# A decoder in one kernel: layer 1's attention with four PSUM banks for maxima and two for scores in place of three and three

## The reference, cut to what matters

```python
qkv = hidden_states @ Wqkv_w.T + Wqkv_b          # b, s, (3, H, HD)
q, k, v = (qkv[:, :, 0], qkv[:, :, 1], qkv[:, :, 2])
softmax_scale = 1.0 / np.float32(np.sqrt(HD))
scores = jnp.einsum('bthd,bshd->bhts', q, k) * softmax_scale
attn = jax.nn.softmax(scores, axis=-1)
ctx = jnp.einsum('bhts,bshd->bthd', attn, v)
return ctx.reshape(b, s, d) @ out_w.T + out_b
```

## Time and profile before

| | us |
|---|---|
| median of 3 runs | 2740.32 |
| lowest and highest | 2739.88, 2743.84 |
| profiled execution, in all | 2736.73 |
| its span | 2735.0 |
| layer 1's attention in it | 1158 to 1461 |
| TensorE busy, share of the span | 2459.4, 90% |
| VectorE busy | 1747.2, 64% |
| ScalarE busy | 1212.6, 44% |

### The profile page before, as it was taken

The page is one execution under the profiler, slowest core; times in us unless marked ns, Lnnn a source line. Parts: engine busy times, 40 slices in busy tenths (PEclk is TensorE's granted clock), DMA queues, the critical chain, the costliest instruction groups (busy, mean ns, idle before and its releaser), DMA issues. The chain is left out here.

```text
span 2735.0 us, 39447 instructions
## 1 busy us (share of the span) xinstructions
PE 2459.4 (90%) x11412; PEld 1779.8 (65%) x11412; DVE 1747.2 (64%) x3684; ACT 1212.6 (44%) x2343; POOL 157.9 (6%) x265
## 2 busy tenths in 40 slices
PE   7999977679999769899999599999999999999579
PEld 5554445457777657654446477777777777777457
DVE  6677756668888662266664666676667666666643
ACT  3566654223333332266663344444444444444321
POOL 0000000010000000100003101010100101010100
PEclk9999998879999979989999799999999999999789
DMA  5522100000000023343320100000000000000101
GB/s 164 167 70 69 52 0 0 17 1 1 0 0 0 4 102 114 120 112 92 84 54 0 54 9 19 4 15 4 15 12 8 12 12 15 4 8 0 40 1 62
DMA packets 71459, 103.69 MB, mean 38 GB/s; under 512 B 14447, under 2 KB 27514, under 8 KB 71262
## 3 DMA queue, kind: packets, MB, share of 16 engines
q1 hardware_dynamic: 71390, 102.82, 12.8%
HBM read 72.90 MB, written 29.88 MB: 38 GB/s over the span
## 5 line engine op out<-in xcount | busy, mean ns | idle before, releaser
L2673 DVE SCALAR_TENSOR_TENSOR x_res<-xa_out_bank,xa_den,x_res 128x512 f32 (+1 forms) x256 | 191.5, 748 | 157.2 <-PE xa_out_bank L2313 157.2
L2582 ACT ACTIVATE xa_pT_hi<-xa_t_bank 128x512 fp32r<-128x512 f32 x256 | 149.5, 597 | 124.8 <-PE xa_t_bank L2450 124.8
L2593 ACT ACTIVATE xa_prob<-xa_prob,xa_nmax 128x512 f32<-128x512 f32 x256 | 182.9, 717 | 30.0 <-DVE xa_nmax L2655 30.0
L2313 PE MATMUL xa_out_bank<-xa_o_w,xa_o_hi 128*128 128x512 f32 x512 | 173.1, 419 | 22.5 <-DVE x_res L2673 20.9
L2637 DVE TENSOR_TENSOR xa_pT_lo<-xa_t_bank,xa_pT_hi 128x512 fp32r<-128x512 f32 x256 | 175.7, 687 | 22.7 <-ACT xa_pT_hi L2582 18.6
L2655 DVE CUSTOM_DVE_ANT_0 xa_prob<-xa_s_bank,xa_mask_bias 128x512 f32<-128x512 f32 x256 | 171.1, 687 | 20.1 <-PE xa_s_bank L2313 10.1
L585 DVE TENSOR_REDUCE l1s_mx<-l1s_max_bank 128x1 f32<-128x512 f32 x256 | 156.3, 682 | 13.2 <-PE l1s_max_bank L447 13.2
L1722 DVE SCALAR_TENSOR_TENSOR ffn_yT<-ffn_y,ffn_ysc,ffn_yT 128x512 f32<-128x512 f32 x176 | 129.3, 748 | 48.9 <-PE ffn_y L1494 48.7
L585 DVE TENSOR_REDUCE l0s_mx<-l0s_max_bank 128x1 f32<-128x512 f32 x256 | 156.0, 682 | 2.8 <-PE l0s_max_bank L447 2.7
L2450 PE MATMUL xa_t_bank<-ident,xa_prob 128*128 128x128 f32 x1024 | 149.8, 274 | 0.1
L572 ACT ACTIVATE l1s_pT<-l1s_score_bank 128x512 f32<-128x512 f32 x256 | 140.0, 601 | 16.3 <-PE l1s_score_bank L466 14.8
(11 more groups left out here) (447 smaller groups left out, 5905.9 us busy)
## 6 DMA issues: line engine op xcount, KB each, us to landing
l0s_q<-l_q SPq DMA_DIRECT2D x96, 128.0 KB, 2.4
l1s_q<-l_q SPq DMA_DIRECT2D x96, 128.0 KB, 3.1
l1s_k<-l_k SPq DMA_DIRECT2D x96, 128.0 KB, 3.3
l0s_k<-l_k SPq DMA_DIRECT2D x96, 64.0 KB, 2.4
x_res<-in_x_dram SPq DMA_DIRECT2D x4, 1024.0 KB, 9.8
l_q<-l_q_hi SPq DMA_DIRECT2D x16, 256.0 KB, 2.6
l_q<-l_q_lo SPq DMA_DIRECT2D x16, 256.0 KB, 3.3
l_q<-l1p_hi SPq DMA_DIRECT2D x16, 256.0 KB, 2.1
```

What stands on the lines that cost most here:

```text
L2313: last = pe.matmul(bank, w, x, start=(m == 0), stop=(m == len(pairs) - 1))
L2582: act.activation(pT_hi[:, kt % (QT - 1), :], t_bank[kt % 2][:], ACT.Copy).then_inc(pT_hi_done, 1)
L2593: act.activation(prob[:, q, :], prob[:, q, :], ACT.Exp, bias=nmax[:, q:q + 1], scale=-1.0, accum_out=den[:, r, 0, q:q + 1]).then_inc(exp_d ...
L2673: dve.scalar_tensor_tensor(xt, out_bank[:], den[:, r, 2, q:q + 1], xt, ALU.mult, ALU.add)\
```

## The change

`PairAttention` gets a number `maxima`, three unless told otherwise; layer 1's attention passes four. It has that many maxima banks and six less that many score banks. Each wait follows its own number: a maximum now waits for the reduction `NM` before it, a score for the exponential `NS` before it. The bank of product j is (8s + j) mod the number of banks, the same as before for three. Layer 0's attention keeps three and three, and the eight banks of PSUM are all in use as before. No instruction is added or removed.

```diff
-    def __init__(self, st, stack, name, q_dram, k_dram, v, per_head, out):
+    def __init__(self, st, stack, name, q_dram, k_dram, v, per_head, out, maxima=3):
...
-        self.max_bank = [ps(f"{name}_max_bank{g}", [P, S]) for g in range(3)]
-        self.score_bank = [ps(f"{name}_score_bank{g}", [P, S]) for g in range(3)]
+        self.NM, self.NS = maxima, 6 - maxima
+        self.max_bank = [ps(f"{name}_max_bank{g}", [P, S]) for g in range(self.NM)]
+        self.score_bank = [ps(f"{name}_score_bank{g}", [P, S]) for g in range(self.NS)]
...
-        reached(pe, self.max_read, 8 * p + j - 2)
-        pe.matmul(self.max_bank[(2 * s + j) % 3][:], self.qs[s][0:self.STK, n, q * P:(q + 1) * P],
+        reached(pe, self.max_read, 8 * p + j - self.NM + 1)
+        pe.matmul(self.max_bank[(8 * s + j) % self.NM][:], self.qs[s][0:self.STK, n, q * P:(q + 1) * P],
...
-        reached(pe, self.exp_done, 8 * p + k - 2)
-        pe.matmul(self.score_bank[(2 * s + k) % 3][:], self.ks[s][0:self.STK + 2, n % self.KN, kt * P:(kt + 1) * P],
+        reached(pe, self.exp_done, 8 * p + k - self.NS + 1)
+        pe.matmul(self.score_bank[(8 * s + k) % self.NS][:], self.ks[s][0:self.STK + 2, n % self.KN, kt * P:(kt + 1) * P],
...
-                act.activation(self.pT[:, n, kt, :], self.score_bank[(2 * s + k) % 3][:], ACT.Exp, scale=HD ** -0.5)\
+                act.activation(self.pT[:, n, kt, :], self.score_bank[(8 * s + k) % self.NS][:], ACT.Exp, scale=HD ** -0.5)\
...
-        dve.tensor_reduce(self.mx[:, j // QT, j % QT:j % QT + 1], self.max_bank[(2 * s + j) % 3][:], AX.X, ALU.max)\
+        dve.tensor_reduce(self.mx[:, j // QT, j % QT:j % QT + 1], self.max_bank[(8 * s + j) % self.NM][:], AX.X, ALU.max)\
...
-        att = PairAttention(st, stack, name, q_dram, k_dram, v, per_head, out)
+        att = PairAttention(st, stack, name, q_dram, k_dram, v, per_head, out, maxima=4)
```

## The result

The changed kernel takes 2747.7 us (median of 10 runs, 2744.2 to 2751.1) against 2740.8 for the kernel before (10 runs, 2738.9 to 2744.0): ratio 1.0025, 95% interval 1.0016 to 1.0034. That is 6.9 us (4.4 to 9.3) slower. The forecast was 2742.5, within 2737 to 2748; the time lies at the range's upper end.

A forecast was written before the change was run, and what follows sets the result against it. The prediction took TensorE's own order as the bound, held in layer 1's loop by maxima waiting for VectorE's reductions. Its terms -1.0+1.4+0.5+1.75-0.4 = +2.2 us, added to the median 2740.32, gave 2742.5 us, range 2737 to 2748.

The forecast's parts named there:

- The wait moves from maxima to scores: Loop steps: maxima's waits for VectorE go or become small; two to three held score loads per step, 1.5 us or less.
- The chain of the two score banks: Steady steps: held load 0.64 us after an exponential's start, next exponential 0.535 later; score 7 starts 3.865 after the first exponential.
- Steps 6 to 29: Layer 1 attention's hardware loop: removed stall replaced almost exactly, -0.04 us a step, -1.0 in all.
- Steps 2 to 5: Layer 1 attention's steps with constant numbers: last score starts at 3.865 for 3.50 us, +0.35 each, +1.4 in all.
- Step 1: Layer 1 attention's step where nothing has to be turned first: last score starts later, +0.5 us.
- The start: Start of layer 1's attention: maximum 7 of pair 1 waits one reduction less, -0.60 to -0.30 us, taken as -0.4.
- Steps 30 and 31: Layer 1 attention's last two steps, without maxima: two score banks delay the last score, +0.87 us each, +1.75 in all.
- The sum: Whole kernel: -1.0+1.4+0.5+1.75-0.4 = +2.2 us, giving 2742.5 us.
- The rival that the stall really goes: Steps with maxima: scores do not bind, -0.59 us in 24 loop steps, about -16 us, 2724; chance 0.03.
- The rival by the clock: Steps 30 and 31: TensorE's clock falls again after looser score stretches; one fall +3.9 us, two +5.6, 2746; chance 0.08.
- The range: Whole kernel's time: 2737 to 2748 us, allowing 3 us for another median.

The follow-up runs named there:

- e9b_half_exp_42: Changed kernel (four maxima, two score banks) with half of layer 1's exponentials left out, 256 of 512 columns; -14.8 us against the kernel before.
- e10b_half_exp_33: Three maxima and three score banks, with half of layer 1's exponentials left out, 256 of 512 columns; -2.5 us against the kernel before.
- e1_after_again: The changed kernel unaltered, run and profiled a second time; +6.3 us against the kernel before.
- e1b_new_text_33: The changed kernel's text with three maxima and three score banks in layer 1, as in the kernel before; -0.2 us against the kernel before.
- e11_filled_tail_42: Changed kernel with sixteen unread matmuls added for TensorE in steps 30 and 31, into idle maxima banks; +2.4 us against the kernel before.
- e5_fixed_tile_42: Changed kernel with layer 1's division written to a fixed-address tile and copied on later by VectorE; +5.6 us against the kernel before.
- e7_six_tail_42: Changed kernel with the scores of steps 30 and 31 put into all six maxima and score banks; -1.5 us against the kernel before.
- e4_fixed_tile_33: Three and three banks, with layer 1's division written to a fixed-address tile and copied on later by VectorE; -6.6 us against the kernel before.

## Why the prediction was partly right and where it failed

- *The wait moves from maxima to scores.* Right, and shown by the two lists of waits. I had expected two or three held loads a step and 1.5 us at most; it is four and 36.1/24 = 1.50 us.
- *The chain of the two score banks* (round of 0.64+0.535). Right to 0.02 us at each gate, though no row of before showed a held score in a step with maxima. e9b_half_exp_42 and e10b_half_exp_33 show that it is this round that binds.
- *Steps 6 to 29*, -1.0 predicted: -0.26, that is -0.01 a step, within the bounds. *Steps 2 to 5*, +1.4: +1.52. *Step 1*, +0.5: from its first maximum to its turn 8.58 us for 8.02, +0.56.
- *The start*, -0.4, was sized too small: -2.31 here, and -2.15 in e1_after_again against e1b_new_text_33 (20.90 for 23.05). The term let the clock rise at the same moment as before. In the changed kernel, e1_after_again, e9b_half_exp_42 and e11_filled_tail_42 it rose 14.9 to 15.3 us behind the first maximum; in e5_fixed_tile_42 and e7_six_tail_42, also with four and two, 18.3 and 17.8 us behind it, and in all eight profiles with another split 18.1 to 18.8. With the late rise e5_fixed_tile_42 has 23.15 for the start and e7_six_tail_42 21.80. Why it rose earlier in four of the six no run shows.
- *Steps 30 and 31*, +1.75: +0.94 and +2.08 here, +0.96 and +0.55 in e1_after_again against e1b_new_text_33. Where only the chain of scores counts it is some 0.9 for each, so that term was right.
- *The sum.* In the traces the terms add up to -2.3+0.6+1.5-0.3+0.9+2.1 = +2.5 us to the last turn, and to +2.8 or +2.1 with the stage behind it. That is near the forecast's +2.2, but partly by luck: the start gained some 2 us more than forecast, and that hid what the clock took in the tail.
- *What the sum lacked* is the clock. Its one term for it, in the start, let it rise when it had; in the tail it took the bubble's own length as the whole cost and put the clock aside as a rival at 0.08. The earlier trace rows already had the kernel before lose 1.7 us to this fall after stretches of 4.28 us, which the change was known to make 5.15. The runs show 10.2 us at the half clock in place of 6.8 (twice each), and e11_filled_tail_42, with the same split and a filled tail, 3.4 us and a time of +2.4, though its score 7 is later than the changed kernel's.
- *What stays open.* One more stretch of 3.4 us at the half clock is 1.7 us by the estimate above, so the sum of terms and clock doesn't reach the medians' +6.9 and +6.3, and some 4 us are in none of the stretches named. For the other kernels too the median and the profiled execution's stretch from first maximum to context attention differ, by -1.3 to +4.1 us. An execution with the late rise of the clock would cost 1 to 2 us more in the start than these two profiles; a trace is of one execution, and how many of the others had it stays open.
- *The rival that the stall really goes*, 0.03: rightly low. The Trainium skill, Perfetto Trace Analysis, section Optimization Strategy, says that a regular bubble can mean too few buffers. e9b_half_exp_42 agrees for this one (8.8 us of waits left of 32.2, score 7 at E+3.30 for 3.89), but taken from a ring that is itself full it bought 0.01 us a step.
- *The rival by the clock* had its place right (the last two steps): the loop kept 1.00 with 1.26 us of idle in 216.75. The Trainium skill, TensorE: Matmul & The Clock Gate, section on a second HAM failure mode, agrees with the trace only in the tail, where step 31 ran at 0.71.
- *The range* held the time, by its upper end.

## What to carry to other kernels

When banks move from one ring to another, write out both rings' rounds from an exponential or reduction to the next held load, and through every engine in the ring; where both are near the bound, look for the late producer (here a division whose destination address was computed in the loop, 0.38 us a step) before sharing the banks out anew. Banks whose user has finished can serve the other ring in the last steps. Where TensorE is loose near the end of a stage, count the clock's fall as a term of the sum and not as a rival, above all if the kernel before already shows one. Compare stretches of the same work in two profiles of each kernel, since here the stages ahead moved a whole span by up to 8 us.

## What the runs showed of the hardware that was not expected

- A VectorE write whose address is computed in the hardware loop started 0.43 us behind the instruction before it (L611 in the changed kernel), while with a constant address it followed at once, in the unrolled steps and in the loop of e4_fixed_tile_33; copied later from a fixed tile, the same destination cost a wait of 0.23 us beside other work.
- More work on TensorE made a kernel faster: sixteen unread matmuls in two steps gave -4.2 us against the changed kernel, uncertain by some 3.5 us (ratios to before 1.0010 and 1.0025), the time at the half clock in the 60 us from there falling from 10.2 to 3.4 us.
- An exponential of 256 columns took some 0.38 us alone, and its hand-over from start to the held load 0.43, against 0.60 and 0.64 for 512 columns: the hand-over shortens with the instruction.
- The clock's rise at the start of the stage came some 3 us earlier behind the first maximum in four of six profiles with four and two (14.9 to 15.3 us) than in all eight with another split (18.1 to 18.8); the start then took 20.7 to 20.9 us, against 22.5 to 23.1 with three and three.
